# Attention over a long context: value product in column halves of TensorE, denominators from paired probabilities, and the row of maxima moved by transfers

## The chip, the core and the metric

The kernel runs on one core of one Trainium2 chip, in one launch. The metric is the device time of the whole program in microseconds (us), as the median of repeated runs. TensorE (PE) multiplies matrices; its weight loads are listed apart (PEld). VectorE (DVE), ScalarE (ACT) and GpSimd (POOL) do the rest of the arithmetic. All transfers are issued by SyncE (SP), in its program order.

## The reference, cut to what matters

Two blocks, each a gated cross-attention and a gated feed-forward part, over 32 batches of 100 rows of width 256. The second block's attention is the largest part. In it every batch attends with 16 heads to 1444 context rows of width 64:

```python
def _L1_xattn_ref(hidden_q, kv_c, Wq, w_kc_q, w_kc_kv, W_qr, W_kr, Wo):
    # q, rotated, and the context, rotated, are compared in 64 dimensions
    # once the weights Wq, w_kc_q, W_qr, W_kr are multiplied out ("absorbed")
    ...
    probs = softmax(scores, axis=-1)          # over 1444 keys, per head and row
    out = probs @ values                      # values = the rotated context, 64 wide
    return out @ (w_kc_kv, Wo)                # also multiplied out
```

So per batch there are 16 x 100 = 1600 query columns of depth 64, 1444 keys, a maximum and a sum over the keys for each query column, and a product with 64 value columns.

## The kernel before

The program is five phases in a row (attention 0, mixture of experts, weights of block 1, attention 1, feed-forward 1); the change is in attention 1 (`phase_l1_attention`, lines 829 to 1390) and in two lines of the phase that prepares its weights. Every engine has its own hand-written program and waits on counting semaphores; nothing is scheduled by a tool.

**Tiles.** Batches are taken in 8 groups of 4 (`NG`, `G`). A batch's 1600 query columns are two chunks of 800 (`CH`, `CQS`), the keys twelve tiles of 120 or 121 (`NT`, `KP`), so a batch has 24 key tiles and a group 96. The variable `r` counts the tiles of a chunk, `c` the chunks, `j` the batches of the group; `at = c * 12 + r` counts a batch's 24 tiles.

**One tile on TensorE** (`scores`, `values`, `beside`): two halves of 400 query columns; for each, scores are two matmuls of type fp32r into one bank of `c_s_ps` (L1340 with the keys and the high part of the queries, L1341 with 65 rows: low part of the queries, and the negated maxima as row 64 against a row of ones). ScalarE takes exp from the bank into `c_p` (L1221, three buffers). Two tiles later (`LAG`) the value product L1352 multiplies `c_val`, 64 value columns and a column of ones, with the two halves of `c_p` into two banks of `c_o_ps`; row 64 of the result is the sum of the probabilities. This product is in fp32, and the trace shows every such matmul as two instructions.

**Maxima.** Ahead of a chunk its scores are computed once more, in coarse form, only for their maxima: seven blocks (six of 128 queries, one of 32), each three matmuls over all keys (L1263) into the three banks of `c_m_ps`, one VectorE reduction (L1084) into `c_mneg`. There is one `c_m_ps`, so a block's matmuls wait for the reduction of the block before. `beside_tile` puts the blocks of a batch's second chunk beside tiles 0, 1, 2, 4, 5, 6, 7 (`LATER`) and those of the next batch's first chunk beside tiles 13, 14, 16, 17, 18, 20, 21 (`NEXT`). Beside tiles 9 and 22 `maxima_row` (L1271) turns the seven columns of negated maxima into one row of `c_m_ps` by seven small matmuls, and ScalarE copies it into row 64 of the queries' low part (L1191); the chunk's first score matmul waits for that.

**Between groups**, a stretch called the head makes the queries of the next four batches: 16 times twelve matmuls (L1290, `wide`), the rotation on VectorE (L1113, four products) and GpSimd (L1028, two sums), and one fp32 product 64 columns wide (L1301, `absorbed`) whose result ScalarE copies twice (L1181) and VectorE subtracts from (L1104). After the head the loop over groups branches back.

**Denominators.** ScalarE drains a chunk's result (L1198); SyncE spreads the row of sums over 100 partitions (L940), VectorE inverts it (L1088), SyncE writes it to memory (L942) and loads it back onto 64 partitions (L945), VectorE multiplies (L1092). GpSimd in a group rotates the next batch's context (L1002, L1004, L1009), copies it into the value tile (L1014) and copies keys (L1019).

```python
LATER, NEXT = (0, 1, 2, 4, 5, 6, 7), (13, 14, 16, 17, 18, 20, 21)
for u, j, c, r in tiles():
    scores(u, j, c, r)
    if len(late) == LAG:
        values(*late.pop(0))
    late.append((u, j, c, r))
    beside(j, c, r)
```

Of the kernel before, what the change touches and what calls it, by code (L numbers as in the profile page):

```python
# [761 lines left out]
def phase_l1_weights(nc, outer, sem, io, m):  # L762

    with ExitStack() as ctx:
# [10 lines left out]
        with nc.Block() as block:  # L775
# [11 lines left out]
            def _(pe):  # L787
# [41 lines left out]
def phase_l1_attention(nc, outer, sem, io, m):  # L829
# [6 lines left out]
    VW = DL + 1  # L836
    with ExitStack() as ctx:
# [12 lines left out]
        rc, rs, rot = sb("c_rc", [HALF, 2, T]), sb("c_rs", [HALF, 2, T]), sb("c_rot", [HALF, 2, 2, T])  # L850
# [3 lines left out]
        val = sb("c_val", [KP, 2, NT, VW])  # L854
        k1 = [sb(f"c_k1{i}", [128, NT * KP], F32R) for i in range(2)]
        k2 = [sb(f"c_k2{i}", [65, NT * KP], F32R) for i in range(2)]
        mneg = sb("c_mneg", [128, NQT, 65], F32R)
        p = sb("c_p", [KP, 3, CQS])
        onum, rdb, ct = sb("c_onum", [65, CQS]), sb("c_rdb", [DL, CQS]), sb("c_ct", [128, CQS])
        den, rden = sb("c_den", [S, CQS // S]), sb("c_rden", [S, CQS // S])  # L860
        s_ps = ps("c_s_ps", [128, 3, 512])
        o_ps = ps("c_o_ps", [128, 2, 512])
        m_ps = ps("c_m_ps", [128, 3, 512])
        m_flat = m_ps[:, :, :].rearrange("p a n -> p (a n)")
        wide_bank = lambda i, a: (s_ps[:, 2 * (i % 2) + a, :] if (i % 2, a) != (1, 1) else o_ps[:, 0, :])
# [9 lines left out]
        maxs_ready, mneg_ready, row_ready, row_copied = count("c_maxs_ready"), count("c_mneg_ready"), count("c_row_ready"), count("c_row_copied")  # L875
        s_ready, exp_ready = count("c_s_ready"), count("c_exp_ready")
        pv_done, on_ready, rden_ready, ct_ready = count("c_pv_done"), count("c_on_ready"), count("c_rden_ready"), count("c_ct_ready")
# [3 lines left out]

        def beside_head(i):
            todo = []
            if i == 3:
                todo.append(("keys", 0))
            if i == 6:
                todo.append(("project", -1))
            if 9 <= i < 9 + NQT:
                todo.append(("max", 0, 0, i - 9))
            return todo  # L890
# [3 lines left out]
        def beside_tile(j, c, r):  # L894
# [3 lines left out]
            if at == 8 and j > 0:  # L898
                todo.append(("project", j - 1))
            if at == 9:  # L900
                todo.append(("row", j, 1))
            if j + 1 < G:
# [4 lines left out]
                if at == 22:  # L907
                    todo.append(("row", j + 1, 0))
# [4 lines left out]
        def tiles():  # L913
            for u in range(NU):
                yield u, u // CT, u // NT % CH, u % NT

        with nc.Block() as block:
            @block.sync
            def _(sp):
# [17 lines left out]
                def spread_denominators(ch):  # L937

                    sp.wait_ge(on_ready, PRIMED + (ch + 1) * 2)
                    sp.dma_start(den[:], onum[DL:DL + 1, :].rearrange("o (p f) -> o p f", p=S)).then_inc(den_loaded, 16)  # L940
# [4 lines left out]
                    sp.dma_start(rdb[:], io["den"].partition_broadcast(DL)).then_inc(rdb_loaded, 16)  # L945

                def group(it, more):
                    for j in range(G):
                        b = it * G + j
                        spread_denominators(b * CH)  # L950
# [4 lines left out]
                        spread_denominators(b * CH + 1)  # L955
# [4 lines left out]
                        sp.wait_ge(x_added, PRIMED + b + 1)  # L960
                        sp.sem_inc(m.carrier, 1)
                        sp.dma_start(io["spill"][bass.ds(b, 1)].rearrange("b s d -> (b s) d"), xr[:, j, :]).then_inc(x_stored, 16)
                        if more:
                            sp.wait_ge(x_stored, 16 * (b + 1))
                            sp.sem_inc(m.carrier, 1)
                            load_residual(b + G, j)
# [11 lines left out]
                load_keys(1)  # L978
                with sp.Fori(0, NG - 1) as it:
                    group(it, True)  # L980
                group(NG - 1, False)
                sp.wait_ge(kv_loaded, B * 48)
# [9 lines left out]
            def _(g):  # L992
# [4 lines left out]
                def rotate_keys(b):  # L997
                    if not isinstance(b, int):
                        g.wait_ge(kt_ready, PRIMED + b * 3)
                    g.wait_ge(kv_loaded, (b + 1) * 48)  # L1000
                    g.wait_ge(v_ready, PRIMED + b)
                    g.tensor_tensor(kva[:], kv[:], kcos[:], ALU.mult).then_inc(kv_roped, 1)  # L1002
                    g.wait_ge(kv_roped, PRIMED + 2 * b + 1)
                    g.tensor_tensor(kv[:], kv[:], ksin[:], ALU.mult).then_inc(kv_roped, 1)  # L1004
                    g.wait_ge(kv_roped, PRIMED + 2 * b + 2)
                    for a in range(2):
                        c0 = slice(a * DL // 2, (a + 1) * DL // 2)
                        c1 = slice((1 - a) * DL // 2, (2 - a) * DL // 2)
# [822 lines left out]
```

## Time and profile before

| | us |
|---|---|
| median of 3 runs (3935.48 to 3946.59) | 3939.77 |
| the profiled execution, whole | 3932.55 |
| its span, first to last instruction | 3930.8 |
| PE busy (90% of the span) | 3538.9 |
| DVE busy (52%) | 2027.9 |
| ACT busy (35%) | 1375.3 |
| POOL busy (21%) | 814.5 |

The page divides the span into 40 slices and gives for each the busy tenths of every engine and the TensorE clock that was granted. Groups of instructions are listed with busy time and mean duration; timelines give start, length and, in brackets, how long the engine stood idle before an instruction and what released it. Matmuls are pipelined and their ends are modelled: consecutive ones overlap, and what counts is the distance from start to start. Attention 1 runs from about 935 us to 3656 us of the span.

### The profile page before, as it was taken

How to read it: one execution, taken by the hardware profiler on the slowest of the kernel's cores; microseconds unless marked ns; L12 is line 12 of the kernel's file. 1: busy time of each engine (PE TensorE's matmuls, PEld its weight loads, DVE VectorE, ACT ScalarE, POOL GpSimd, SP SyncE). 2: the span in 40 equal slices, each digit the busy share in tenths (PEclk: the TensorE clock that was granted, in tenths of full speed). 3: DMA queues.
4: the chain of work that ended last, by engine and by line, in shares of the span. 5: the costliest groups of instructions: out<-in, count | busy, mean ns of one | idle time of the engine just before them, and what ended most of it. 6: DMA issues, size and time to landing. Idle time of an engine off the chain costs nothing. (4 is left out here: it accounts for less than half of the span.)

```text
span 3930.8 us, 51787 instructions
## 1 busy us (share of the span) xinstructions
PE 3538.9 (90%) x16584; PEld 2434.5 (62%) x16592; DVE 2027.9 (52%) x3166; ACT 1375.3 (35%) x2778; POOL 814.5 (21%) x678
## 2 busy tenths in 40 slices
PE   6999799996999999999999999999999999999244
PEld 5777688884666566656656665665665666566122
DVE  5777644444543644544364454445445444542588
ACT  1333222221334243234324323433432343334256
POOL 0000122222210410311131131122014012210367
PEclk9999799997999999999999999999999999999666
DMA  3000100003000000000000000000000000000200
GB/s 94 0 0 0 41 0 0 0 11 86 7 18 15 9 17 17 13 8 19 17 5 17 18 12 14 15 17 3 17 19 11 15 13 19 3 16 9 76 11 23
DMA packets 65315, 69.40 MB, mean 18 GB/s; under 512 B 23464, under 2 KB 55560, under 8 KB 65026
## 3 DMA queue, kind: packets, MB, share of 16 engines
q1 hardware_dynamic: 65090, 66.55, 6.1%
q8 instruction: 123, 2.02, 0.2%
q14 instruction: 102, 0.84, 0.1%
HBM read 56.30 MB, written 10.04 MB: 17 GB/s over the span
## 5 line engine op out<-in xcount | busy, mean ns | idle before, releaser
L1352 PE MATMUL c_o_ps<-c_p,c_val 120*65 120x400 f32 (+1 forms) x3072 | 1156.9, 499 | 2.0 <-ACT c_onum L1198 2.0
L1084 DVE TENSOR_REDUCE c_mneg<-c_m_ps 128x1 fp32r<-128x1452 f32 (+1 forms) x448 | 746.7, 1667 | 748.7 <-PE c_m_ps L1263 748.0
L1221 ACT ACTIVATE c_p<-c_s_ps 120x400 f32<-120x400 f32 (+1 forms) x1536 | 691.2, 501 | 1041.2 <-PE c_s_ps L1341 1033.2
L1340 PE MATMUL c_s_ps<-c_q,c_k 128*120 128x400 f32 (+1 forms) x1536 | 630.5, 410 | 30.4 <-issue 28.1
L1352 PEld LDWEIGHTS c_o_ps<-c_p,c_val 120*65 120x65 f32 (+1 forms) x3072 | 420.6, 137 | 354.2 <-issue 315.6
L1341 PE MATMUL c_s_ps<-c_q,c_k 65*120 65x400 f32 (+1 forms) x1536 | 538.3, 350 | 0.0
L1263 PE MATMUL c_m_ps<-c_k,c_q 128*128 128x484 f32 (+1 forms) x1344 | 456.3, 448 | 19.0 <-DVE c_mneg L1084 9.8
L1263 PEld LDWEIGHTS c_m_ps<-c_k,c_q 128*128 128x128 f32 (+1 forms) x1344 | 231.0, 181 | 223.9 <-DVE c_mneg L1084 113.4
L1028 POOL TENSOR_TENSOR c_rot<-c_rc,c_rs 96x400 f32<-96x400 f32 x256 | 262.1, 1044 | 508.0 <-DVE c_rs L1113 265.1
L1340 PEld LDWEIGHTS c_s_ps<-c_q,c_k 128*120 128x120 f32 (+1 forms) x1536 | 285.7, 186 | 103.3 <-issue 76.5
L1341 PEld LDWEIGHTS c_s_ps<-c_q,c_k 65*120 65x120 f32 (+1 forms) x1536 | 286.9, 187 | 56.6 <-issue 39.1
L1181 ACT ACTIVATE c_q<-c_o_ps 64x400 fp32r<-64x400 f32 x256 | 127.4, 498 | 477.8 <-PE c_o_ps L1301 474.7
L1002 POOL TENSOR_TENSOR c_kva<-c_kv,c_kcos 121x768 f32<-121x768 f32 x32 | 58.1, 1816 | 1025.1 <-DMA c_kv<-in_ctx 1021.8
L1290 PE MATMUL c_s_ps<-c_xt,l_a 128*96 128x400 f32 x1152 | 239.3, 353 | 1.8 <-DVE c_xt L1072 1.8
L709 PE MATMUL b_gu_ps<-b_xt,l_a 128*128 128x400 f32 x1056 | 213.8, 354 | 11.2 <-DVE b_gated L556 11.2
L1301 PE MATMUL c_o_ps<-c_rot,l_mqk 96*64 96x400 f32 x512 | 202.6, 519 | 22.7 <-DVE c_q L1104 22.7
L1290 PEld LDWEIGHTS c_s_ps<-c_xt,l_a 128*96 128x96 f32 x1152 | 183.6, 163 | 57.0 <-DVE c_rs L1113 23.2
L709 PEld LDWEIGHTS b_gu_ps<-b_xt,l_a 128*128 128x128 f32 x1056 | 193.2, 192 | 18.1 <-DVE b_gated L556 18.0
L1113 DVE TENSOR_TENSOR c_rc<-c_s_ps,c_qcos 96x400 f32<-96x400 f32 x192 | 108.9, 567 | 156.7 <-PE c_s_ps L1290 121.3
L522 POOL TENSOR_TENSOR b_act_lo<-b_act,b_act_hi 128x400 fp32r<-128x400 f32 x88 | 91.7, 1046 | 322.5 <-ACT b_act_hi L664 322.5
L1078 DVE TENSOR_TENSOR c_k<-c_m_ps,c_k 64x484 fp32r<-64x484 f32 x96 | 57.3, 648 | 186.3 <-ACT c_k L1187 186.0
L1019 POOL CAST c_k<-c_k 64x1452 fp32r<-64x1452 f32 x32 | 44.5, 1390 | 488.4 <-ACT c_k L1187 488.4
(220 smaller groups left out, 4273.0 us busy)
## 6 DMA issues: line engine op xcount, KB each, us to landing
c_rdb<-l_denominators SPq DMA_DIRECT2D x64, 200.0 KB, 3.3
c_kv<-in_ctx SPq DMA_DIRECT2D x32, 360.0 KB
x_rows<-in_x SPq DMA_DIRECT2D x4, 800.0 KB
x_spill<-x_rows SPq DMA_DIRECT2D x1, 3200.0 KB
c_xa<-x_spill SPq DMA_DIRECT2D x8, 400.0 KB
c_xr<-x_spill SPq DMA_DIRECT2D x32, 100.0 KB
x_spill<-c_xr SPq DMA_DIRECT2D x32, 100.0 KB
d_rows<-x_spill SPq DMA_DIRECT2D x5, 640.0 KB, 11.3
```

What stands on the lines that cost most here:

```text
L709: mm = pe.matmul(gu_ps[:, t % 2, j, 0:T], w[wi][:, k, t * 128:(t + 1) * 128], xt[x][:, k, :], start=(i == 0 and k == 0), stop=(i == 2 and ...
L1028: g.tensor_tensor(rot[:, i % 2, a, :], rc[:, a, :], rs[:, a, :], ALU.add).then_inc(rot_ready, 1)
L1084: v.tensor_reduce(mneg[0:n, t, DL:DL + 1], m_ps[0:n, :, 0:4 * KP], AX.XY, ALU.max, negate=True).then_inc(mneg_ready, 1)
L1113: v.tensor_tensor(dst[:, a, :].rearrange("p (b s) -> p b s", b=G), wide_bank(i, half)[0:HALF, 0:T].rearrange("p (b s) -> p b s", b=G), tab ...
L1181: a.activation(q1[half * DL:(half + 1) * DL, :, cols], o_ps[0:DL, 1, 0:T].rearrange("p (b s) -> p b s", b=G), ACT.Copy).then_inc(q1_ready, 1)
L1221: a.activation(p[0:k, u % 3, i * CQS // 2:(i + 1) * CQS // 2], s_ps[0:k, (2 * u + i) % 3, 0:CQS // 2], ACT.Exp).then_inc(exp_ready, 1)
L1263: mm = pe.matmul(m_ps[0:n, k, 0:4 * KP], q1[:, j, c * CQS + t * 128:c * CQS + t * 128 + n], k1[j % 2][:, k * 4 * KP:(k + 1) * 4 * KP], sta ...
L1290: mm = pe.matmul(wide_bank(i, a)[0:HALF, 0:T], m.a[w][:, k, HEADS[i], a * HALF:(a + 1) * HALF], xt[x][:, k, :], start=(q == 0 and k == 0), ...
L1301: mm = pe.matmul(o_ps[0:DL, 1, 0:T], m.mqk[:, a, HEADS[i], :], rot[:, i % 2, a, :], start=(a == 0), stop=(a == 1))
L1340: pe.matmul(o, k1[j % 2][:, r * KP:r * KP + k], q1[:, j, cols], start=True, stop=False)
L1341: mm = pe.matmul(o, k2[j % 2][:, r * KP:r * KP + k], q2[:, j, cols], start=False, stop=True)
L1352: mm = pe.matmul(o_ps[0:VW, i, 0:CQS // 2], val[0:k, j % 2, r, :], p[0:k, u % 3, i * CQS // 2:(i + 1) * CQS // 2], start=(r == 0), stop=(r ...
```

## The change

- **Value product.** The column of ones leaves `c_val`. The two halves of 400 query columns go to PSUM partitions 0 to 63 and 64 to 127 of a single bank, so each matmul names one column half of the array.
- **Sums.** GpSimd adds the probabilities of tiles 2q and 2q+1 into `c_psum` (two buffers). After every second value product TensorE multiplies `c_psum` with 32 columns of ones, four matmuls of 200 query columns at PSUM partitions 0, 32, 64, 96 of a bank `c_d_ps`. ScalarE's exp into a buffer of `c_p` now also waits for the pair's addition.
- **GpSimd's order.** The rotation of the next context is cut into four parts, which stand between additions.
- **Row of maxima.** `maxima_row` and its copy go. `c_mneg` holds plain columns, and SyncE moves them with seven transfers per chunk straight into row 64 of the queries' low part; the chunk's first score matmul waits for all of them (`row_loaded`).
- **Head.** The absorbed products are made for two heads at once, in the two column halves; the maxima blocks stand beside heads 4, 6, 7, 9, 10, 11, 12 (before: 9 to 15), keys beside head 1, the projection beside head 5. Four copies on ScalarE and two subtractions on VectorE follow each pair.
- **Denominators.** The sums come from four partitions (four transfers), the inverses go back in two; the final product is 128 x 400, and head pairs are regrouped in the weights for it. The projection of the batch before stands beside tile 9 (before: 8).

```diff
+                def load_row(ch, j, c):
+                    sp.wait_ge(mneg_ready, PRIMED + (ch + 1) * NQT)
+                    sp.sem_inc(m.carrier, 1)
+                    for t in range(NQT):
+                        sp.dma_start(q2[DL:DL + 1, j, c * CQS + t * 128:c * CQS + t * 128 + QT[t]].bitcast(F32), mneg[0:QT[t], c, t:t + 1].bitcast(F32)).then_inc(row_loaded, 16)
...
+                def add_pair(it, j, q):
+                    n = it * NU // 2 + j * CT // 2 + q
+                    g.wait_ge(exp_ready, PRIMED + 4 * (n + 1))
+                    if (j, q) >= (0, 2):
+                        g.wait_ge(den_done, PRIMED + n - 1)
...
+                    g.tensor_tensor(psum[0:k, q % 2, :], p[0:k, u % 3, :], p[0:k, (u + 1) % 3, :], ALU.add).then_inc(psum_ready, 1)
...
                             if u >= 3:
                                 a.wait_ge(pv_done, PRIMED + n - 2)
+                                a.wait_ge(psum_ready, PRIMED + it * NU // 2 + (u - 3) // 2 + 1)
...
-                            pe.wait_ge(row_copied, PRIMED + (it * G + j) * CH + c + 1)
+                            pe.wait_ge(row_loaded, 16 * NQT * ((it * G + j) * CH + c + 1))
...
                         for i in range(2):
-                            mm = pe.matmul(o_ps[0:VW, i, 0:CQS // 2], val[0:k, j % 2, r, :], p[0:k, u % 3, i * CQS // 2:(i + 1) * CQS // 2],
-                                           start=(r == 0), stop=(r == NT - 1))
-                        mm.then_inc(pv_done, 1)
+                            mm = pe.matmul(o_ps[i * DL:(i + 1) * DL, 0:HALFQ], val[0:k, j % 2, r, :], p[0:k, u % 3, i * HALFQ:(i + 1) * HALFQ],
+                                      start=(r == 0), stop=(r == NT - 1))
+                            if i == 1:
+                                mm.then_inc(pv_done, 1)
+                        if r % 2 == 1:
+                            pe.wait_ge(psum_ready, PRIMED + it * NU // 2 + u // 2 + 1)
+                            for q in range(4):
+                                mm = pe.matmul(d_ps[q * 32:(q + 1) * 32, 0:QUART], ones[0:k, :], psum[0:k, u // 2 % 2, q * QUART:(q + 1) * QUART],
+                                               start=(r == 1), stop=(r == NT - 1))
+                            mm.then_inc(den_done, 1)
...
-                            mm = pe.matmul(o_ps[0:DL, 1, 0:T], m.mqk[:, a, HEADS[i], :], rot[:, i % 2, a, :], start=(a == 0), stop=(a == 1))
+                            for half in range(2):
+                                i = 2 * pair + half
+                                mm = pe.matmul(d_ps[half * DL:(half + 1) * DL, 0:T], m.mqk[:, a, HEADS[i], :], rot[:, i % 4, a, :], start=(a == 0), stop=(a == 1))
```

TensorE before, from the value product of tile 20 (issued in tile 22) to the scores of tile 23:

```order
L1352 MATMUL c_o_ps<-c_p,c_val 65x400 x2
L1269 ISA
L1271 MATMUL c_m_ps<-identr,c_mneg 65x128 x6
L1271 MATMUL c_m_ps<-identr,c_mneg 65x32
L1337 REGISTER_ALU
L1340 MATMUL c_s_ps<-c_q,c_k 120x400
L1341 MATMUL c_s_ps<-c_q,c_k 120x400
```

TensorE after, from the last maxima block, beside tile 21, to the scores of tile 23 (L1308 is the maxima, L1378 and L1379 the scores, L1390 the values):

```order
L1308 MATMUL c_m_ps<-c_k,c_q 32x484 x3
L1375 REGISTER_ALU
L1378 MATMUL c_s_ps<-c_q,c_k 120x400
L1379 MATMUL c_s_ps<-c_q,c_k 120x400
L1375 REGISTER_ALU
L1378 MATMUL c_s_ps<-c_q,c_k 120x400
L1379 MATMUL c_s_ps<-c_q,c_k 120x400
L1384 ISA
L1390 MATMUL c_o_ps<-c_p,c_val 64x400 x2
L1375 REGISTER_ALU
L1378 MATMUL c_s_ps<-c_q,c_k 120x400
```

The seven matmuls of the row are gone, and nothing stands in their place.

TensorE after, the end of tile 23 and the first score matmul of the next batch, the one that waits for the row (L1397 is the product with ones):

```order
L1390 MATMUL c_o_ps<-c_p,c_val 64x400 x2
L1395 REGISTER_ALU
L1397 MATMUL c_d_ps<-c_psum,c_ones 32x200 x4
L1369 ISA
L1371 REGISTER_ALU
L1375 REGISTER_ALU
L1378 MATMUL c_s_ps<-c_q,c_k 121x400
```

Between the last maxima block and this matmul stand the scores and values of two tiles and one product with ones; the value products of tiles 22 and 23 stand behind it.

SyncE before, the second chunk's denominators and the load of a later context:

```order
L940 DMA c_den<-c_onum 100x1x8
L941 REGISTER_ALU
L942 DMA l_denominators<-c_rden 100x8
L943 REGISTER_ALU
L945 DMA c_rdb<-l_denominators 64x800
L957 ISA
L932 ISA
L932 DMA c_kv<-in_ctx 120x768
```

SyncE after, the same place:

```order
L946 DMA c_den<-c_oden 25x1x8 x4
L948 DMA l_denominators<-c_rden 100x8
L949 REGISTER_ALU
L952 DMA c_rdb<-l_denominators 64x400 x2
L956 ISA
L959 DMA c_q<-c_mneg 1x128x1 x6
L959 DMA c_q<-c_mneg 1x32x1
L992 ISA
L937 ISA
L937 DMA c_kv<-in_ctx 120x768
```

The load of the context now stands behind the row's seven transfers, and so behind the last maximum of the next batch's first chunk.

## Rows read from the trace of the kernel before

**Rows 1.** The page: span, and granted TensorE clock by slice in tenths.

```profile
span 3930.8 us, 51787 instructions
...
PEclk9999799997999999999999999999999999999666
```

**Rows 2.** Timeline, PE, in a group: start us, length us, engine, line.

```profile
1085.21 1.51 PE L1352 MATMUL c_o_ps<-c_p,c_val 120*65 120x400 f32 x4
...
1089.14 0.97 PE L1263 MATMUL c_m_ps<-c_k,c_q 128*128 128x484 f32 x3
...
1091.88 0.97 PE L1263 MATMUL c_m_ps<-c_k,c_q 128*128 128x484 f32 x3
```

**Rows 3.** Timeline, ACT, two tiles, the second without a maxima block.

```profile
1059.58 0.90 ACT L1221 ACTIVATE c_p<-c_s_ps 121x400 f32<-121x400 f32 x2
1062.32 0.90 ACT L1221 ACTIVATE c_p<-c_s_ps 121x400 f32<-121x400 f32 x2 [1.84 <-PE c_s_ps L1341]
1064.40 0.90 ACT L1221 ACTIVATE c_p<-c_s_ps 120x400 f32<-120x400 f32 x2 [1.19 <-PE c_s_ps L1341]
```

**Rows 4.** Timeline, DVE, a reduction beside the tiles of rows 2.

```profile
1090.15 1.67 DVE L1084 TENSOR_REDUCE c_mneg<-c_m_ps 128x1 fp32r<-128x1452 f32 x1 [1.06 <-PE c_m_ps L1263]
```

**Rows 5.** Timeline, PE, the weights phase: fp32 matmuls in alternating column halves.

```profile
928.65 1.08 PE L806 MATMUL w_b_ps<-w_wo,w_kckv 128*64 128x256 f32 x8
```

**Rows 6.** Timeline, PE, one head of the sixteen between groups.

```profile
2009.70 1.25 PE L1290 MATMUL c_s_ps<-c_xt,l_a 128*96 128x400 f32 x6
...
2011.98 1.56 PE L1301 MATMUL c_o_ps<-c_rot,l_mqk 96*64 96x400 f32 x4
2013.46 0.93 PE L1263 MATMUL c_m_ps<-c_k,c_q 128*128 128x484 f32 x3
2014.23 0.35 PE L1290 MATMUL c_s_ps<-c_xt,l_a 128*96 128x400 f32 x1
```

**Rows 7.** Timeline, all engines, the last maxima block of a chunk and its row.

```profile
1078.80 0.96 PE L1263 MATMUL c_m_ps<-c_k,c_q 128*32 128x484 f32 x3
1079.80 1.66 DVE L1084 TENSOR_REDUCE c_mneg<-c_m_ps 32x1 fp32r<-32x1452 f32 x1 [1.06 <-PE c_m_ps L1263]
1081.51 0.85 PE L1271 MATMUL c_m_ps<-identr,c_mneg 128*65 128x128 f32 x7
1082.29 0.44 PE L1340 MATMUL c_s_ps<-c_q,c_k 128*120 128x400 f32 x1
```

**Rows 8.** Timelines of SP and DVE at the phase's end.

```profile
3639.56 0.77 SPq L940 DMA_DIRECT2D c_den<-c_onum  x1
3641.92 0.29 SPq L942 DMA_DIRECT2D l_denominators<-c_rden  x1
3643.20 0.47 SPq L945 DMA_DIRECT2D c_rdb<-l_denominators  x1
...
3641.69 0.20 DVE L1088 RECIPROCAL c_rden<-c_den 100x8 f32<-100x8 f32 x1 [18.40 <-DMA c_den<-c_onum]
```

**Rows 9.** Stretches around a head's end: length, busy us of each engine, clock.

```profile
1350.00:1357.00 7.00, 2.19 (x11) 1.03 (x11) 1.13 (x2) 2.66 (x5) 5.00 (x5) 1.00 0.02 5
1357.00:1367.00 10.00, 7.96 (x20) 6.21 (x21) 3.34 (x2) 4.20 (x7) 0.00 (x0) 0.50 0.01 3
```

**Rows 10.** Timeline, PE, the same head's end.

```profile
1351.61 1.53 PE L1301 MATMUL c_o_ps<-c_rot,l_mqk 96*64 96x400 f32 x4 [1.80 <-DVE c_q L1104]
...
1358.61 0.69 PE L1340 MATMUL c_s_ps<-c_q,c_k 128*121 128x400 f32 x1 [4.81 <-issue]
```

**Rows 11.** Groups by line, POOL: count, busy us, mean ns, idle before.

```profile
L1004 POOL TENSOR_TENSOR c_kv<-c_kv,c_ksin 121x768 f32<-121x768 f32 x32 | 72.4, 2263 | 2.5
...
L1002 POOL TENSOR_TENSOR c_kva<-c_kv,c_kcos 121x768 f32<-121x768 f32 x32 | 58.1, 1816 | 1025.1 <-DMA c_kv<-in_ctx 1021.8 <-issue 3.3
```

**Rows 12.** Timeline, DVE, one head with a maxima block.

```profile
2003.12 0.57 DVE L1113 TENSOR_TENSOR c_rc<-c_s_ps,c_qcos 96x400 f32<-96x400 f32 x1
...
2006.07 1.65 DVE L1084 TENSOR_REDUCE c_mneg<-c_m_ps 128x1 fp32r<-128x1452 f32 x1
```

More of the change, by code:

```diff
@@ L897, in beside_tile @@
                 todo.append(("max", j, 1, LATER.index(at)))
-            if at == 8 and j > 0:
+            if at == 9 and j > 0:
                 todo.append(("project", j - 1))
-            if at == 9:
-                todo.append(("row", j, 1))
             if j + 1 < G:
@@ L959, in group @@
                             load_keys(b + 2)
[L960 to L966, printed above, removed]
                 load_rows(0)
@@ L1034, in group @@
                         b = it * G + j
-                        if more or j + 1 < G:
-                            rotate_keys(b + 1)
-                            g.wait_ge(pv_done, PRIMED + b * CT)
-                            place_values(b + 1, (j + 1) % 2)
-                        if j + 1 < G:
-                            copy_keys(b + 1, j + 1)
-                        elif more:
-                            deviation(it + 1)
+                        for q in range(CT // 2):
+                            add_pair(it, j, q)
+                            if more or j + 1 < G:
+                                if q < 4:
+                                    rotate_keys(b + 1, q)
+                                if q == 4:
+                                    g.wait_ge(pv_done, PRIMED + b * CT)
+                                    place_values(b + 1, (j + 1) % 2)
+                            if q == 7 and j + 1 < G:
+                                copy_keys(b + 1, j + 1)
+                            if q == 5 and j + 1 == G and more:
+                                deviation(it + 1)
                 deviation(0)
                 g.wait_ge(t_loaded, 16 * 4)
-                rotate_keys(0)
+                for i in range(4):
+                    rotate_keys(0, i)
                 place_values(0, 0)
@@ L1175, in _, with copy_queries @@
             def _(a):
-                def copy_queries(gi, i):
-                    n, h = gi * H + i, HEADS[i]
-                    cols = slice((h % 2) * CQS + (h // 2) * S, (h % 2) * CQS + (h // 2 + 1) * S)
-                    a.wait_ge(q_ps_ready, PRIMED + n + 1)
-                    for half in range(2):
-                        a.activation(q1[half * DL:(half + 1) * DL, :, cols], o_ps[0:DL, 1, 0:T].rearrange("p (b s) -> p b s", b=G),
-                                     ACT.Copy).then_inc(q1_ready, 1)
+                def copy_queries(gi, pair):
+                    a.wait_ge(q_ps_ready, PRIMED + gi * (H // 2) + pair + 1)
+                    a.sem_inc(m.carrier, 1)
+                    for i in range(2):
+                        for half in range(2):
+                            a.activation(q1[half * DL:(half + 1) * DL, :, head_cols(2 * pair + i)],
+                                         d_ps[i * DL:(i + 1) * DL, 0:T].rearrange("p (b s) -> p b s", b=G), ACT.Copy).then_inc(q1_ready, 1)
                 def copy_keys(b, j):
```

228 lines of the change are left out of this document (125 added, 103 removed).

## The prediction

> **What bounds the kernel now.** I read the page first, then the timeline of TensorE inside a group, then the timelines of the engines that answer to it, and last the stretches at a head's end. The span is 3930.8 us, and TensorE runs at its full clock, 2.4 GHz, in nearly all of the attention [rows 1]. Inside a group TensorE is the bound. A tile without a maxima block comes 2.08 us after the one before, a tile with one 2.74 us (1062.32 to 1064.40, 1059.58 to 1062.32) [rows 3]. Both are filled by matmuls alone. The value product's four instructions last 1.51 us, a single one 0.50, so they start (1.51 - 0.50) / 3 = 0.335 us apart and take 4 x 0.335 = 1.34 us [rows 2]; an fp32r matmul of 400 columns takes (1.25 - 0.35) / 5 = 0.18 us [rows 6], so the four score matmuls take 0.74. Sum 2.08. A block's three matmuls of 484 columns add 3 x 0.22 = 0.66.
>
> Beside this stands a second limit that happens to be as long. In tiles with a block VectorE works 1.67 us and idles 1.06 us for the next block's matmuls [rows 4]; 2.73 us is the shortest distance between two blocks as long as there is one `c_m_ps`, whatever TensorE saves.
>
> A batch of 24 tiles with 14 blocks and two rows is then 24 x 2.08 + 14 x 0.66 + 2 x 0.78 plus projection and keys, which stay. In the head, one of the 16 heads with a block takes 4.53 us (2009.70 to 2014.23) [rows 6].
>
> **The value product.** Two halves run side by side only if the array takes both at once. The trace has such matmuls, fp32 in alternating column halves: eight instructions of 256 columns in 1.08 us [rows 5]. In sequence they would take 7 x 0.335 x 256/400 + 0.38 = 1.9 us; pairwise, 3 x 0.215 + 0.38 = 1.03. So they overlap fully, and the product falls from 1.34 to 0.67 us a tile.
>
> What this costs shows in the head. There a product 64 columns wide (L1301) stands between full-width ones. A head's matmuls sum to 12 x 0.18 + 4 x 0.335 + 0.66 = 4.19 us if 0.182 is used for the first; the cadence is 4.53 [rows 6]. The missing 0.34 us lies before and after L1301: its first instruction starts 2011.98, and the next block at 2013.46 is 1.48 us later and not 1.34. In the tile of rows 2 no such time is missing. I charge 0.34 us for each trip from full width to a half and back. The Trainium skill, "TensorEngine Tiling (Array Packing)", Key Properties, says that changing the tiling mode drains TensorE. By that rule the trip has its price in every tile of the group, as charged; without it, the sum would be that of rival 2.
>
> The product with ones: four matmuls of 200 columns, each two instructions, are 8 x 0.168 = 1.34 us in sequence and 0.335 with four side by side. Quarters don't occur in the trace; I take 0.335 by the halves' row, with 1.34 as the other end. Going from halves to quarters I charge 0.14, half a trip.
>
> An even tile then costs 0.74 + 0.67 + 0.34 = 1.75 us, an odd one 1.75 + 0.335 + 0.14 = 2.22, on average 1.98 against 2.08. With a block 2.40 or 2.88; but where a block follows directly on a block (9 times a batch, 4 of them even) the limit of 2.73 us holds. A batch: -24 x 0.10 = -2.4, +4 x 0.34 = +1.4, two rows of 0.78 us gone (1081.51 to 1082.29) [rows 7] -1.6: together -2.6. The last batch of a group has 7 blocks and one row: -2.5. Per group -10.3, for 8 groups **-82 us**. (From +10 per batch, quarters in sequence, to -9, no trips; both are rivals.)
>
> **GpSimd.** 768 columns take 1.82 to 2.26 us [rows 11]; an addition of 800 columns is then 1.9 to 2.4. exp of tile 2q+3 waits for it, and it starts with the end of exp 2q+1: 0.90 [rows 3] + 0.1 + 1.9 + 0.1 = 3.0 us, at most 3.5, against two tiles of together 3.97 at least. It stays hidden by 0.5 to 1 us. The rotation's longest part, 2.26, fits behind an addition because its pairs of tiles last over 5 us. I take 0.
>
> **The head.** Eight products in halves of 1.34 + 0.34 take the place of sixteen: -8 x 1.68 = -13.4 us at most. VectorE gives some back: with a block its head is 4 x 0.48 + 0.5 + 1.65 = 4.1 us [rows 12], and four copies of 0.5 on ScalarE now stand between a product and the subtractions. For heads 9 to 12, with a block each, I reckon 9.3 us per pair where TensorE alone needs 7.4, so +3.9; keys, projection and the end, where one product with 2 us of copies replaces two with 1, another +1.5. That is -8 per head (0 to -13), for 8 **-64 us**. The 4.81 us in which TensorE branches back to the loop's start [rows 10] stay.
>
> **The row of maxima.** This is where the change loses. The last block beside tile 21 starts at M; its reduction starts 1.00 later and lasts 1.66 (1078.80, 1079.80) [rows 7], so the maxima are there at M + 2.7. Now SyncE issues seven transfers. No row shows one like it: single elements from 128 partitions into one. Nearest is L940, the only one between partitions of SBUF: issue 0.77 us, and its data is used 2.13 us after its start, 1.36 after the issue's end [rows 8]; at the other end L942, 0.29 of issue and 1.28 until SyncE goes on. So the row is complete 0.1 + 7 x 0.77 + 1.36 = 6.9 us after the maxima, or 0.1 + 7 x 0.29 + 1.0 = 3.1. I take 6.9. TensorE reaches the next batch's first scores at M + 0.66 + 1.75 + 2.22 = M + 4.6. It waits until M + 9.6: **5.0 us** (1.2 with the short issue), and behind the waiting matmul are queued both open value products and the next block, so nothing fills the gap. ScalarE and VectorE wait with it. This happens at 3 batch borders of each group, 24 times: +120 us (+29). The other rows are hidden: that of the second chunk is complete 9.6 us after its last block's start, beside tile 7, and tiles 8 to 11 with the keys keep TensorE busy for 0.66 + 2 x 3.97 + 1.2 = 9.8 us or more until tile 12; that of the head has three heads and the tail behind it.
>
> Such a gap has a second price. Before a head's end TensorE worked 2.19 us of 7, and the clock then stood at 0.50, that is 1.2 GHz, for the next 10 us, though the engine was busy 8 of them [rows 9]. A gap of 5 us is like the 4.81 of [rows 10]. After the gap 6 to 8 us at half clock lose 3 to 4, some of it in the slack under the 2.73: I take 3.0 (0 to 5), 24 times +72 us.
>
> A transfer's cost by the Trainium skill, "DMA: Bandwidth & Descriptors", Anatomy of one DMA, is about 2.0 us, most of it the receipt of the last write; with only that once and issues of no length the row would be complete about 2 us after the maxima and the gap closed. The trace's 1.36 agrees with the receipt, but has the issues of 0.77 in front, and there are seven.
>
> Denominators: three issues more per chunk, 2.3 us; they are used at r = 3 and 6 and hidden; at the very end of the phase +2 us, inside rounding.
>
> **Sum.** -82 - 64 + 120 + 72 = +46 us. The profiled execution took 3932.6, so 3979; it lies 7 us below the median of the runs, and I forecast **3982**. Over 0.3% (12 us) can be told from no change.
>
> **Rivals.**
> 1. *The transfers are quick.* SyncE issues each in 0.29; gap 1.2 us, in which I let the clock stay up (shorter than either gap of [rows 10]). -82 - 64 + 29 = -117: 3820. For it: L942 also reads a column of partitions. Against: its far side is memory, in rows of 32 bytes.
> 2. *The trip costs nothing* where halves follow full width in every tile. A tile averages 1.57, blocks in a row stay at 2.73: -9.4 per batch in place of -2.6, -218 more for 32 batches; the gap grows by 0.8 us (+19): 3780. Against it: every head shows 0.34.
> 3. *Slower than the forecast: quarters run in sequence.* +1.0 us per pair, 384 pairs: +386 and less gap: 4340. It decides the sign if a product with ones takes over 0.2 us more than its 0.335. Against it: rows 5.
> 4. *GpSimd becomes the bound.* If additions take 3 us beside VectorE, exp waits 0.6 us per pair: +150 on the forecast, 4130.
>
> **How the numbers follow.** Forecast 0.62, with own range 3920 to 4080 (issue 0.5 to 1.0 us, clock 0 to 5 us); rival 1 0.20; rival 2 0.10; rival 3 0.04; rival 4 0.04. Range 3800 to 4090, which leaves out most of rivals 2 to 4. Faster: rivals 1 and 2 and 0.05 of the forecast, 0.35; same 0.08; slower 0.57.
>
> **What would show it.** Value products of two instructions' length, 0.67 us, and distances of 2.2 and 1.75 between plain tiles in turn; 2.73 between blocks; TensorE idle about 5 us before the first scores of three batches per group, released by the transfers into the queries' tile; seven issues of 0.8; clock slices of 7 to 9 tenths in the attention. Wrong would be: no such gap, tiles of 1.6, a product with ones over 0.6, or exp released by GpSimd.

## The result, and the profile after

| | before | changed |
|---|---|---|
| median of 6 runs | 3937.6 us | **3963.9 us** |
| runs | 3933.7 to 3946.6 | 3959.7 to 3973.1 |
| profiled execution (span) | 3932.6 (3930.8) | 3959.7 (3957.5) |

The change makes the kernel slower by 0.7%: ratio 1.0069, 95% interval 1.0053 to 1.0086. Forecast were 3982 us and "slower", so the sign and the chain of causes came out, with the sizes of the head, the gap and the clock off.

The page of the changed kernel, span and granted clock by slice, beside [rows 1]: slices of 8 tenths stand among the 9s of the attention.

```profile
span 3957.5 us, 59524 instructions
...
PEclk8999799997899899989989998998999999899566
```

Its waits of TensorE: engine and line, what it waited for, us in total, times, longest. The first line here is new, and is the row of maxima: 94.8 / 24 = 3.95 us at each of the three borders of batches inside each of the eight groups.

```profile
PE c_s_ps L1378 <- DMA c_q<-c_mneg: 94.8, 24, 4.7
PE c_m_ps L1308 <- DVE c_mneg L1135: 63.6, 129, 2.6
PE c_s_ps L1378 <- issue: 46.4, 6, 7.9
...
PE c_d_ps L1342 <- DVE c_q L1156: 28.7, 8, 3.7
```

Two plain tiles on TensorE's timeline, to be held against [rows 2] and [rows 3]. They are 1.75 us (2275.94 to 2277.69) and 2.23 us (to 2279.92) long, where both were 2.08. The value product, L1390, takes 0.82 us from its first start to the next matmul and not 4 x 0.335: its halves run side by side (2 x 0.335), and 0.15 us is lost in it. Another 0.10 us stands before it (0.28 between starts, not 0.18) and 0.10 behind the first scores.

```profile
2275.94 0.45 PE L1378 MATMUL c_s_ps<-c_q,c_k 128*121 128x400 f32 x1
...
2276.59 0.35 PE L1379 MATMUL c_s_ps<-c_q,c_k 65*121 65x400 f32 x1
2276.87 0.89 PE L1390 MATMUL c_o_ps<-c_p,c_val 120*64 120x400 f32 x4
2277.69 0.44 PE L1378 MATMUL c_s_ps<-c_q,c_k 128*121 128x400 f32 x1
2277.97 0.35 PE L1379 MATMUL c_s_ps<-c_q,c_k 65*121 65x400 f32 x1
...
2278.62 0.89 PE L1390 MATMUL c_o_ps<-c_p,c_val 120*64 120x400 f32 x4
2279.44 0.55 PE L1397 MATMUL c_d_ps<-c_psum,c_ones 120*32 120x200 f32 x8
2279.92 0.44 PE L1378 MATMUL c_s_ps<-c_q,c_k 128*121 128x400 f32 x1
```

A border of batches, in three timelines. TensorE starts the last block at 2164.88, is done with its last product at 2169.5 and starts the next scores at 2173.35:

```profile
2164.88 0.84 PE L1308 MATMUL c_m_ps<-c_k,c_q 128*32 128x484 f32 x3
...
2168.94 0.55 PE L1397 MATMUL c_d_ps<-c_psum,c_ones 120*32 120x200 f32 x8
2173.35 0.44 PE L1378 MATMUL c_s_ps<-c_q,c_k 128*121 128x400 f32 x1 [3.87 <-DMA c_q<-c_mneg]
...
2174.27 1.59 PE L1390 MATMUL c_o_ps<-c_p,c_val 120*64 120x400 f32 x4
2175.79 1.58 PE L1308 MATMUL c_m_ps<-c_k,c_q 128*128 128x484 f32 x3
```

VectorE has the last maximum at 2167.41, and stands for 10 us after it:

```profile
2165.75 1.66 DVE L1135 TENSOR_REDUCE c_mneg<-c_m_ps 32x1 fp32r<-32x1452 f32 x1 [1.14 <-PE c_m_ps L1308]
2177.40 1.67 DVE L1135 TENSOR_REDUCE c_mneg<-c_m_ps 128x1 fp32r<-128x1452 f32 x1 [10.00 <-PE c_m_ps L1308]
```

SyncE issues the seven transfers from 2167.50 to 2171.88 (0.63 us each), and the row is used 1.47 us later. At 22 of the 24 borders the seven issues take 4.38 us like here, at the other two 4.92 and 5.22:

```profile
2167.50 4.38 SPq L959 DMA_DIRECT2D c_q<-c_mneg  x7
```

The same border in stretches (length, busy us of PE, PEld, DVE, ACT, POOL, then the granted clock): nothing but GpSimd works in the gap, and behind it the clock is low, a mean of 0.67 over 5.2 us, a part of them at 1.2 GHz. There the value product takes 1.59 us for 0.89 and the block 1.58 for 0.92.

```profile
2169.50:2173.30 3.80, 0.00 (x0) 0.00 (x0) 0.00 (x0) 0.00 (x0) 1.41 (x1) 1.00 0.11 8
2173.30:2178.50 5.20, 5.15 (x17) 3.09 (x19) 1.10 (x1) 1.32 (x4) 0.00 (x0) 0.67 0.23 66
2178.50:2184.50 6.00, 5.78 (x34) 2.98 (x30) 3.54 (x3) 2.95 (x8) 3.69 (x2) 1.00 0.01 2
```

In the gap of this border the clock is still 1.00. That is so at 6 of the 24 borders; at the other 18 it falls 1.0 to 2.4 us before TensorE starts again. The border with the longest gap (4.75 us, 2100.10 to 2104.84), in stretches:

```profile
2098.50:2104.80 6.30, 1.60 (x14) 0.35 (x12) 0.00 (x0) 0.90 (x2) 1.88 (x1) 0.83 0.14 7
2104.80:2110.00 5.20, 5.16 (x15) 3.18 (x15) 0.39 (x1) 1.01 (x2) 0.00 (x0) 0.55 0.22 64
```

GpSimd's additions by line (count, busy us, mean ns, idle before and its cause), the answer to [rows 11]: 1.90 us each, and always idle in front of one.

```profile
L1077 POOL TENSOR_TENSOR c_psum<-c_p 120x800 f32<-120x800 f32 (+1 forms) x384 | 729.8, 1901 | 1219.3 <-ACT c_p L1268 1219.3
```

The head, beside [rows 6]. TensorE first: a block waits 2.61 us for the block before it, and the clock falls behind that wait too (1.57 us for 0.93, 2.20 for 1.25).

```profile
1315.22 0.93 PE L1308 MATMUL c_m_ps<-c_k,c_q 128*128 128x484 f32 x3
1315.99 2.35 PE L1327 MATMUL c_s_ps<-c_xt,l_a 128*96 128x400 f32 x12
1320.95 1.57 PE L1308 MATMUL c_m_ps<-c_k,c_q 128*128 128x484 f32 x3 [2.61 <-DVE c_mneg L1135]
1322.31 2.20 PE L1327 MATMUL c_s_ps<-c_xt,l_a 128*96 128x400 f32 x6
```

VectorE in the same time: the matmuls at 1315.22 are done by 1316.2, but their reduction stands behind the rotations of two heads and the pair's subtractions and comes at 1319.22. VectorE has nearly no idle time in these 7 us.

```profile
1313.83 0.57 DVE L1165 TENSOR_TENSOR c_rc<-c_s_ps,c_qcos 96x400 f32<-96x400 f32 x1
...
1318.03 1.16 DVE L1156 TENSOR_TENSOR c_q<-c_d_ps,c_q 64x400 fp32r<-64x400 f32 x2
1319.22 1.67 DVE L1135 TENSOR_REDUCE c_mneg<-c_m_ps 128x1 fp32r<-128x1452 f32 x1
1320.92 0.57 DVE L1165 TENSOR_TENSOR c_rc<-c_s_ps,c_qcos 96x400 f32<-96x400 f32 x1
```

The head's end, beside [rows 10]: the last pair's product waits 3.57 us and takes 2.94 us where the others take 1.56, and 7.86 us without TensorE, not 4.81, lie between it and the group.

```profile
1346.50 2.94 PE L1342 MATMUL c_d_ps<-c_rot,l_mqk 96*64 96x400 f32 x8 [3.57 <-DVE c_q L1156]
1357.30 0.69 PE L1378 MATMUL c_s_ps<-c_q,c_k 128*121 128x400 f32 x1 [7.86 <-issue]
```

### The profile page after: what moved, and what is told of

Same layout as the page of the kernel before. It is cut to its first block and busy times, and to the rows that moved or that the text cites. A ratio compares the mean times of both kernels' runs of the same rounds, so it can differ in the third digit from the quotient of the medians.

```text
span 3957.5 us, 59524 instructions
## 1 busy us (share of the span) xinstructions
PE 3390.5 (86%) x19216; PEld 2147.7 (54%) x19216; DVE 1996.0 (50%) x3165; ACT 1314.5 (33%) x2714; POOL 1525.3 (39%) x1062
## 5 line engine op out<-in xcount | busy, mean ns | idle before, releaser
L1077 POOL TENSOR_TENSOR c_psum<-c_p 120x800 f32<-120x800 f32 (+1 forms) x384 | 729.8, 1901 | 1219.3 <-ACT c_p L1268 1219.3
L1135 DVE TENSOR_REDUCE c_mneg<-c_m_ps 128x1 fp32r<-128x1452 f32 (+1 forms) x448 | 747.1, 1668 | 887.7 <-PE c_m_ps L1308 887.0
L1378 PE MATMUL c_s_ps<-c_q,c_k 128*120 128x400 f32 (+1 forms) x1536 | 590.1, 384 | 149.2 <-DMA c_q<-c_mneg 94.8
L1390 PE MATMUL c_o_ps<-c_p,c_val 120*64 120x400 f32 (+1 forms) x3072 | 704.5, 539 | 0.1
L1379 PE MATMUL c_s_ps<-c_q,c_k 65*120 65x400 f32 (+1 forms) x1536 | 549.4, 358 | 0.0
L1308 PE MATMUL c_m_ps<-c_k,c_q 128*128 128x484 f32 (+1 forms) x1344 | 435.8, 435 | 63.6 <-DVE c_mneg L1135 63.6
L1378 PEld LDWEIGHTS c_s_ps<-c_q,c_k 128*120 128x120 f32 (+1 forms) x1536 | 294.9, 192 | 331.9 <-issue 210.1
L1308 PEld LDWEIGHTS c_m_ps<-c_k,c_q 128*128 128x128 f32 (+1 forms) x1344 | 218.4, 189 | 324.5 <-DVE c_mneg L1135 189.4
L1379 PEld LDWEIGHTS c_s_ps<-c_q,c_k 65*120 65x120 f32 (+1 forms) x1536 | 295.7, 193 | 19.0
L1390 PEld LDWEIGHTS c_o_ps<-c_p,c_val 120*64 120x64 f32 (+1 forms) x3072 | 155.6, 137 | 215.8 <-issue 201.2
L1231 ACT ACTIVATE c_q<-c_d_ps 64x400 fp32r<-64x400 f32 x256 | 127.7, 499 | 397.1 <-PE c_d_ps L1342 392.4
L1397 PE MATMUL c_d_ps<-c_psum,c_ones 120*32 120x200 f32 (+1 forms) x3072 | 210.5, 345 | 0.7 <-POOL c_psum L1077 0.3
L1397 PEld LDWEIGHTS c_d_ps<-c_psum,c_ones 120*32 120x32 f32 (+1 forms) x3072 | 60.4, 108 | 241.2 <-issue 234.9
L1753 PE MATMUL d_y_ps<-d_w,d_hqt 128*128 128x256 bf16 x200 | 43.5, 392 | 109.9 <-ACT d_hqt L1702 109.9
```

What stands on the lines that cost most here:

```text
L1077: g.tensor_tensor(psum[0:k, q % 2, :], p[0:k, u % 3, :], p[0:k, (u + 1) % 3, :], ALU.add).then_inc(psum_ready, 1)
L1135: v.tensor_reduce(mneg[0:n, c, t:t + 1], m_ps[0:n, :, 0:4 * KP], AX.XY, ALU.max, negate=True).then_inc(mneg_ready, 1)
L1231: a.activation(q1[half * DL:(half + 1) * DL, :, head_cols(2 * pair + i)], d_ps[i * DL:(i + 1) * DL, 0:T].rearrange("p (b s) -> p b s", b=G ...
L1308: mm = pe.matmul(m_ps[0:n, k, 0:4 * KP], q1[:, j, c * CQS + t * 128:c * CQS + t * 128 + n], k1[j % 2][:, k * 4 * KP:(k + 1) * 4 * KP], sta ...
L1378: pe.matmul(o, k1[j % 2][:, r * KP:r * KP + k], q1[:, j, cols], start=True, stop=False)
L1379: mm = pe.matmul(o, k2[j % 2][:, r * KP:r * KP + k], q2[:, j, cols], start=False, stop=True)
```

## The experiments

The theory: tiles and head gain, and the row of maxima gives more than that back, because seven issues in a row come only after the last maximum; the idle time of TensorE that follows costs its length and a lower clock behind it. The rivals: another wait would be there without it; the transfer's landing is what takes long; the long tiles after the gap are engines being refilled; GpSimd or the changes of tiling are the cost. All kernels stand on the changed one unless another is named. Ratios are to the kernel before, run on the same chip; its median there is 3935 to 3940 us, so times of two experiments can be some 4 us apart without a cause. Lengths of tiles and heads are between starts on TensorE, as means over the groups.

**The last blocks earlier.** The row has two tiles more to hide behind.

```
-        ..., NEXT = (0, 1, 2, 4, 5, 6, 7), (13, 14, 16, 17, 18, 20, 21)
+        ..., NEXT = (0, 1, 2, 4, 5, 6, 7), (13, 14, 15, 16, 17, 18, 19)
```

> The blocks of the next batch's maxima stand beside tiles 13 to 19 in place of 13 to 21, so that the row's seven transfers (5.0 us of issues, 2.0 us to land, in the changed kernel's trace) have four tiles to hide behind. Theory A (TensorE stands 4.0 us at each of 24 batch borders because the transfers start only after the last maximum, and loses about 1.6 us more to a lower clock afterwards, 5.6 us each): -24 x 5.6 = -135 us, less some 0.5 us a batch for two more blocks that follow on a block; 3964 - 135 + 12 = 3840 us (3815 to 3865). Theory B (the stop only takes up slack that the reductions or the keys would need anyway): another wait of similar length takes its place, 3920 to 3965 us.

Measured 3835.6 us (3826.1 to 3839.5), ratio 0.9737 (0.9715 to 0.9759). Of TensorE's waits for the row 8 are left, 6.6 us together, and no other takes the gap's place; theory B falls.

**Each transfer when its maximum is there.**

```
-                    sp.wait_ge(mneg_ready, PRIMED + (ch + 1) * NQT)
-                    sp.sem_inc(m.carrier, 1)
                     for t in range(NQT):
+                        sp.wait_ge(mneg_ready, PRIMED + ch * NQT + t + 1)
+                        sp.sem_inc(m.carrier, 1)
                         sp.dma_start(q2[...], mneg[...]).then_inc(row_loaded, 16)
```

> SyncE issues each of the row's seven transfers as soon as its own maximum is there, not all seven after the last. Theory A (the stop of 4.0 us is made of the 5.0 us that seven issues take one after the other): after the last maximum one issue of 0.7 us and a landing of 2.0 us remain, 4.3 us less than now, the stop is gone: 3964 - 135 = 3830 us (3810 to 3860). Theory C (it is made of the landing time, or of SyncE being late for another reason): the stop stays, 3940 to 3965 us.

Measured 3832.0 us (3829.4 to 3839.3), ratio 0.9738 (0.9720 to 0.9756). The order of the blocks is untouched, so it was the issues after the last maximum. A border on TensorE's timeline, to be held against the one above: 2.4 us from the first scores of one tile to the next batch's.

```profile
2053.42 0.45 PE L1378 MATMUL c_s_ps<-c_q,c_k 128*120 128x400 f32 x1
...
2055.17 0.55 PE L1397 MATMUL c_d_ps<-c_psum,c_ones 120*32 120x200 f32 x8
2055.82 0.44 PE L1378 MATMUL c_s_ps<-c_q,c_k 128*121 128x400 f32 x1
```

**Fourteen transfers of half the length.** The waits for the row count 14 of them.

```
+                        n = QT[t] // 2
+                        for h in range(2):
-                        sp.dma_start(q2[... t * 128:... + QT[t]], mneg[0:QT[t], ...])
+                            sp.dma_start(q2[... t * 128 + h * n:... + n], mneg[h * n:(h + 1) * n, ...])
```

> Each of the row's seven transfers is cut in two of half the length (14 issues, the same elements). If the issue has a fixed price of 0.7 us each, the stop grows by 4.9 us at 24 borders, +118 us and some clock: 4085 us or more. If the price goes by elements (5.5 ns for each single element), the stop stays and the time is 3964 us (3955 to 3985).

Measured 4145.3 us (4132.6 to 4157.3), ratio 1.0525 (1.0492 to 1.0557): even more than the fixed price gives. SyncE's and TensorE's timelines of a border: 14 issues take 8.82 us, 0.63 each like the seven before, so between 128 and 64 elements the length of a transfer does not count, only their number. (21 of the 24 borders have this length, the longest has 9.52.)

```profile
1966.55 8.82 SPq L961 DMA_DIRECT2D c_q<-c_mneg  x14
```

```profile
1976.89 0.69 PE L1380 MATMUL c_s_ps<-c_q,c_k 128*121 128x400 f32 x1 [8.34 <-DMA c_q<-c_mneg]
```

The 24 tiles at the borders last 10.6 us, not 6.2, which is +106; 8 x 6.1 more go at the row of the second chunk in each group's first batch, which was hidden before, and about 20 at that row in the other batches and in the tiles behind the gaps: +175 of the +181. TensorE's waits for the transfers are 42 now, 233.2 us together, and not 24.

**The row by TensorE again.** This part alone is undone: `maxima_row` and `copy_row` come back as in the kernel before, and the transfers go.

> The changed kernel with this one part undone: the row of maxima is again turned by seven matmuls of TensorE and copied by ScalarE, as before the change. Theory A: the 24 stops and their clock go (-135 us), 64 row products of 0.78 us come back (+50 us): 3880 us (3860 to 3900), faster than the kernel before (3938 us) by the halves and the head pairs alone. Theory B (the loss lies elsewhere in the change): 3950 us or more.

Measured 3895.5 us (3892.2 to 3901.5), ratio 0.9895 (0.9876 to 0.9914). Without the transfers the change is 1.1% faster than before. The row products cost 15 us more than I reckoned: with the row beside tile 9, the projection waits for ScalarE's copy (the tile lasts 7.2 us, not 5.57, 24 times).

**Matmuls in the gap.** Twenty are put in front of the wait; the row comes no sooner.

```
+                        if r == 0 and c == 0 and j > 0:
+                            pe.wait_ge(exp_ready, PRIMED + 2 * it * NU + 2 * u - 2)
+                            for _ in range(20):
+                                pe.matmul(s_ps[0:k, 2 * u % 3, 0:CQS // 2], k1[...], q1[...], start=True, stop=True)
                         if r == 0:
                             pe.wait_ge(row_loaded, 16 * NQT * (...))
```

> The changed kernel with 20 more matmuls of 400 columns (3.6 us, their result is overwritten) in front of TensorE's wait for the row at the 24 borders inside groups: the wait stays, but TensorE works through it. If the tiles behind the wait are long (4.13 and 3.2 to 3.46 us in place of 2.30 and 2.90) because the clock has been lowered by the idle time, they become 2.3 and 2.9 and 24 x 2.2 = 53 us go: 3964 - 53 = 3911 us (3900 to 3925). If they are long because ScalarE and VectorE have to be filled again, 3964 us.

Measured 3917.9 us (3903.3 to 3921.4), ratio 0.9959 (0.9943 to 0.9974): 46 us less than the changed kernel, by nothing but useless work. The first tile after the border now takes 2.49 us, where the changed kernel has 4.34 (3.79 to 4.53), and the second 2.90, where it has 3.10; the expectation's 4.13 and 2.30 are not the distances between starts. The granted clock of the 5.2 us behind the wait is 1.00, and the value product there is back to 0.89:

```profile
2077.44 3.90 PE L1371 MATMUL c_s_ps<-c_q,c_k 128*121 128x400 f32 x20
2081.74 0.42 PE L1382 MATMUL c_s_ps<-c_q,c_k 128*121 128x400 f32 x1 [0.40 <-DMA c_q<-c_mneg]
...
2082.64 0.89 PE L1394 MATMUL c_o_ps<-c_p,c_val 120*64 120x400 f32 x4
```

ScalarE (5.5 us) and VectorE (9.0 us) stood idle here as in the changed kernel (5.2 and 10.0), so the refilling theory falls and the clock is left.

**GpSimd's additions cut to 8 columns.** `psum[0:k, q % 2, 0:8]` and the like in `add_pair`, on top of the piecewise row. The sums of the other 792 columns are left out (`c_psum` is filled with ones), so the denominators are not the reference's.

> On e2_row_piecewise: GpSimd adds 8 of the 800 columns of each pair of tiles (the other sums are left out, so the denominators are not the reference's); all waits and the product with ones stay. If the additions are hidden: 3832 us (3822 to 3840). If GpSimd holds exp up, or slows VectorE's reductions beside it: 3810 us or less, with reductions shorter than 1.66 us.

Measured 3838.3 us (3834.8 to 3840.8), ratio 0.9752 (0.9715 to 0.9789), against 0.9738 with the additions. By line, they now take 0.20 us each and VectorE's reductions are 1668 ns as they were. Neither is the bound, and the one does not slow the other.

```profile
L1135 DVE TENSOR_REDUCE c_mneg<-c_m_ps 128x1 fp32r<-128x1452 f32 (+1 forms) x448 | 747.2, 1668 | 749.6 <-PE c_m_ps L1309 748.9
...
L1077 POOL TENSOR_TENSOR c_psum<-c_p 120x8 f32<-120x8 f32 (+1 forms) x384 | 77.0, 201 | 1712.7 <-ACT c_p L1269 1712.7
```

**Value products of two tiles together**, on the piecewise row. `c_p` has four buffers, and the waits for them follow.

```
-        p, psum = sb("c_p", [KP, 3, CQS]), ...
+        p, psum = sb("c_p", [KP, 4, CQS]), ...
-                        if len(late) == LAG:
+                        if len(late) == 3:
                             values(*late.pop(0))
+                            values(*late.pop(0))
```

> On e2_row_piecewise: the value products of two tiles stand together in front of their product with ones (one trip from full width to halves and quarters for two tiles, not one for each; a fourth buffer for the probabilities makes it possible). If a trip costs 0.34 us, the seven of twelve pairs of tiles in which TensorE is the bound get 0.34 us shorter, 2.4 us a batch, 2.9 in a group's last, 8 x (3 x 2.4 + 2.9) = -81 us: 3832 - 81 = 3751 us (3740 to 3790), and a plain pair takes 3.6 us in place of 3.97. If the trip costs nothing and tiles are long for another reason: 3832 us; if the bunched products hold exp up, over 3850 us.

Measured 3861.0 us (3846.8 to 3864.5), ratio 0.9799 (0.9758 to 0.9840): a miss, 29 us slower than with the piecewise row alone (24 by the ratios). A plain pair is 3.83 us long, not 3.97, so 0.14 of the 0.34 is gained. TensorE's timeline of such a pair: the eight value matmuls take 1.49 us, 1.34 and one loss of 0.15. But two scores now start 0.28 us apart where 0.18 is usual (1264.40, 1264.68, 1264.96), since the fourth half of the scores has to wait for exp of the first (ScalarE ends it at 1264.62). That is 0.2 us.

```profile
1264.40 0.34 PE L1379 MATMUL c_s_ps<-c_q,c_k 65*120 65x400 f32 x1
1264.68 0.44 PE L1378 MATMUL c_s_ps<-c_q,c_k 128*120 128x400 f32 x1
1264.96 0.35 PE L1379 MATMUL c_s_ps<-c_q,c_k 65*120 65x400 f32 x1
1265.24 1.56 PE L1390 MATMUL c_o_ps<-c_p,c_val 120*64 120x400 f32 x8
1266.73 0.55 PE L1397 MATMUL c_d_ps<-c_psum,c_ones 120*32 120x200 f32 x8
```

The time is lost where the even tile of a pair has a block right behind another one. It has no value product now and can't be shorter for it: TensorE waits 1.03 us there for the reduction, and the tile keeps its 2.69 us, while the odd tile carries both products. Tiles 6 and 7 take 2.69 + 3.48 = 6.17 us where they were 2.69 + 2.81 = 5.50, and 2 and 3, 14 and 15, 18 and 19 take 5.49 for 4.82. The pairs 4 and 5, 16 and 17, 20 and 21, whose even tile does not follow a block, gain 0.34 each. The price of a trip as such is not isolated by this run; the sums agree with it, no more. The two delays of 0.10 us beside a value product stand in these rows at a wait between full-width scores too, so not all of the 0.35 need be the change of tiling.

**The head's blocks spread**, on the piecewise row.

```
-        HEAD_MAX, HEAD_PROJECT = (4, 6, 7, 9, 10, 11, 12), 5
+        HEAD_MAX, HEAD_PROJECT = (4, 6, 7, 9, 11, 13, 15), 5
```

> On e2_row_piecewise: the head's seven blocks stand beside heads 4, 6, 7, 9, 11, 13, 15 in place of 4, 6, 7, 9, 10, 11, 12. If the head gained 3 us and not 8 because VectorE is the bound where each head has a block (4.0 + 5.1 us a pair of heads, and ScalarE's copies in front of its subtractions), the wide products of heads 9 to 12 get shorter and the last blocks fill the tail: -3 us a head, -24 us, 3808 us (3800 to 3820). If the loss is in the head's end alone (the last product waits 3.6 us for the pair before it): 3832 us, or a little more.

Measured 3785.7 us (3777.0 to 3788.6), ratio 0.9613 (0.9575 to 0.9652): 46 us gained where I expected 24. From the first wide product of a head to the sixteenth it is 53.5 us, where it is 61.6 with the piecewise row alone and 60.3 in the changed kernel; from group to group 76.1 us, not 83.0. In the pairs with one block TensorE does not wait for a reduction, and its clock stays up (1.00 from 1312 to 1329). Its timeline, a pair in 3.58 + 1.26 + 1.56 + 0.93 less the overlaps, 7.08 us:

```profile
1314.79 0.93 PE L1308 MATMUL c_m_ps<-c_k,c_q 128*128 128x484 f32 x3
1315.77 3.58 PE L1327 MATMUL c_s_ps<-c_xt,l_a 128*96 128x400 f32 x18
...
1320.37 1.56 PE L1342 MATMUL c_d_ps<-c_rot,l_mqk 96*64 96x400 f32 x8
1321.87 0.93 PE L1308 MATMUL c_m_ps<-c_k,c_q 128*128 128x484 f32 x3
```

**The projection later in the head**, `HEAD_PROJECT = 8`, and the normalisation beside head 6.

> As e7_head_spread, and the projection stands beside head 8 in place of 5, its normalisation beside head 6. Head 5 lasts 8.3 us where the same head without a projection lasts 4.0; the projection itself is 3.3, so 1.0 us of waits goes; and VectorE, which idles 0.9 and 1.8 us there, has its work where TensorE has its own: -2 us a head, 3808 - 16 = 3792 us. If those waits only move: 3808 us.

Measured 3796.8 us (3790.4 to 3802.8), ratio 0.9652 (0.9613 to 0.9692). A miss: no gain. Head 5 falls from 8.11 to 3.77 us, but heads 7 and 8 rise from 4.54 + 2.19 to 5.69 + 7.37, of which the projection that moved is 3.3. The waits moved and grew: 78.1 us from group to group, not 76.1.

**The waits at the head's end behind the jump**, on the spread head.

```
                     absorbed(H // 2 - 1)
-                    pe.wait_ge(q1_ready, PRIMED + 2 * (gi + 1) * H)
-                    pe.wait_ge(q2_ready, PRIMED + (gi + 1) * H)
...
                     late = []
+                    pe.wait_ge(q1_ready, PRIMED + 2 * (it + 1) * H)
+                    pe.wait_ge(q2_ready, PRIMED + (it + 1) * H)
```

> On e7_head_spread: TensorE's two waits for the last pair's queries stand behind the loop's jump, at the group's start, not in front of it. In e7 TensorE idles 7.7 us between the head's last product and the group's first scores. If that is 3.3 us of copies and subtractions and then 4.4 us of jump, one behind the other, they now overlap: -3.3 us at 7 heads, 3786 - 23 = 3763 us (3755 to 3775). If the first scores wait for something later (the row of maxima), 3786 us.

Measured **3757.0 us** (3748.7 to 3760.1), ratio 0.9546 (0.9530 to 0.9562): the best version, 4.5% faster than before and 5.2% faster than the change as it was made. TensorE's timeline: 3.92 us idle and a released wait, in place of 7.7 with the jump behind the copies.

```profile
1324.19 2.93 PE L1342 MATMUL c_d_ps<-c_rot,l_mqk 96*64 96x400 f32 x8 [3.55 <-POOL c_rot L1063]
1331.04 0.69 PE L1376 MATMUL c_s_ps<-c_q,c_k 128*121 128x400 f32 x1 [3.92 <-DVE c_q L1156]
```

## Why the prediction was right, and where it was off

| term | forecast | measured |
|---|---|---|
| tiles of the groups | -82 | -86 |
| head | -64 | -29 |
| gap at the borders | +120 | +95 |
| clock behind the gap | +72 | +46 to +49 |
| sum | +46 | +26 to +29; medians +26 |

*Tiles.* From a group's first tile to its last the kernel before takes 251.7 us, the one with the piecewise row, which has no gap, 240.9: -10.8 a group, -10.3 forecast. Plain tiles of 1.75 and 2.23 us were forecast to 0.01 us. Quarters run side by side and each tile pays the trip: rivals 2 and 3 are out. By the Trainium skill ("TensorEngine Tiling (Array Packing)", Key Properties) a change of tiling drains the engine. The trace agrees: 0.35 us more than the matmuls' own time in each tile that has a value product between full-width ones. That all of it is the drain is not shown.

*Gap.* The chain was as forecast: TensorE at the wait at M + 4.6, and nothing behind it that could run. The size is 3.95 us on average and not 5.0, because an issue takes 0.63 us and not the 0.77 of the nearest row, [rows 8]: 7 x 0.14 = 1.0. With 0.29, rival 1, there would be a gap of about 1.6 us. I had the right mechanism from a row for another pattern of addresses, and that its price came within 0.14 us was luck in part; the same row's 1.36 us from issue's end to use is 1.5 on average. The section that the prediction cites for 2.0 us (the Trainium skill, "DMA: Bandwidth & Descriptors", Anatomy of one DMA) describes transfers that GpSimd issues, and here SyncE issues them.

*Clock.* Forecast 3.0 us a border, measured 46 / 24 = 1.9 by the filled gap, and 1.8 + 0.2 = 2.0 by the two tiles behind it (4.34 for 2.51, 3.10 for 2.90). I let the low level last 6 to 8 us as at the head's end [rows 9]; behind this gap it is gone within 6, at the six borders where it begins only behind the gap within 5.

*Head.* From a group's last tile to the next one's first it is 82.2 us, 85.6 before, and the first head is 5.3 us shorter: 7 x 3.4 + 5.3 = 29. This step was off most. I summed VectorE's work and reckoned 9.3 us for a pair with two blocks; heads 9 and 10 take 10.5 and 11 and 12 take 11.1, 3.0 of the 4.6 us that are missing in each head. The sum of the work was right, its order was not in it: a reduction that stands behind the rotations of two heads holds up the next block, the next wide product stands behind that block, and the clock falls behind the wait. Spreading the blocks brings 6.9 us a head, 46 us in all, so more had been lost there than the 35 by which the term fell short. The end costs 17.5 us from the sixteenth wide product to the group, 16.1 before: +1.4, where 1.5 was reckoned for it, keys and projection together. Its parts were not foreseen: I let the 4.81 us stay, and they are 7.86, and the last product takes 2.94 us for 1.56.

*GpSimd.* Costed at nothing, and it is nothing: 1.90 us per addition, 3838 us without the additions and 3832 with.

Too high a gain in the head (35 us) and too high a loss at the borders (48 to 51 us) came near to cancelling, which was luck. The forecast's 3982 is nearer the measured 3964 than its terms deserve.

## What to carry to other kernels

A transfer that takes the place of a matmul and a copy frees the engines and moves the work to a queue where each issue has its own price, here 0.63 us for 64 elements as for 128; issue each piece when its data is there, and keep the last one's landing ahead of its reader. When TensorE has to wait, count its length and the matmuls at half clock behind it, here 1.9 us for a gap of 4. In a stage where two engines are nearly even, sum the work in the order in which it is queued, and ask what the last instruction of each round stands behind: moving three numbers of such a table was worth 46 us here, over half of what the halves and quarters bring.

## What the hardware showed that I had not expected

Seven issues of 128 single elements from 128 partitions into one took 4.38 us at most borders, and fourteen of 64 took 8.82 us: 0.63 each. Behind gaps of 3.8 to 4.8 us the low clock came at all 24 borders, and its price is paid with TensorE already at work: at 6 of the 24 borders the clock is 1.00 in the whole gap and falls about 1 us behind it, and the first tile lasts 3.8 us; at the other 18 it falls in the gap, and the first tile lasts 4.5. Where the gap is filled the matmuls behind it have their full-clock length. A gap of 8.3 us, with fourteen transfers, has hardly more behind it than one of 3.9: the two tiles after it last 7.90 us and 7.44, where they last 5.41 without a gap.
